# A decoder layer on one core: the first transfers in another order and on two queues, and the orders of all engines anew

## The chip, the cores and the metric

One core of a Trainium2 chip runs the whole program. The metric is the device time in microseconds (us). TensorE is called PE, VectorE DVE, ScalarE ACT, GpSimd POOL and SyncE SP, as in the profile.

## The reference

32 sequences of 128 tokens with 512 channels pass through one decoder layer in float32:

```python
x = x + _L0_attn_ref(_layernorm(x), ...)          # linear attention with decay, 32 heads of 16
x = x + _L0_xattn_ref(_layernorm(x), ctx, ctx)    # cross attention, 32 query heads, 8 key/value heads
x = x + _L0_ffn_ref(_layernorm(x), ...)           # feed-forward part with block-quantised operands
```

The attention part forms xx = (previous token - token), mixes it with a weight per channel into four inputs (`mix_r`, `mix_k`, `mix_v`, `mix_g`), projects each with a 512x512 weight, multiplies the scores of a head with powers of its decay, normalises the result per head, multiplies it with a gate silu(g) and projects it with Wo. The feed-forward part goes 512 to 2048 to 512 through a tanh-gelu. Its activations and both weights are quantised in blocks of 32 values with a shared exponent.

## The kernel before

One sequence is one tile of 128 tokens. All engines run at once, each through its own straight list of steps, and wait for each other with semaphores (`e.wait_ge`). The lists are written out by hand for sequences 0 to about 10 and for the last five. In between stands `for n in range(11, 27)` on every engine, so 16 turns of a loop in which one turn works on several sequences at different depths (the loading for n, the attention of n-1 and n-2, cross attention of n-3 and n-4, feed-forward of n-5 and n-6). The order of a list is the schedule: an engine stands still at a step whose wait isn't met, even when a later one could run.

Steps that matter here:
- `load_x`, `load_turned`: a sequence into `xin`, and the same transposed into `xt`.
- `stats_q(n)`, `norm_mv("q", n)` (DVE, L1623 to L1634), `rstd_log`, `rstd_exp` (ACT, L2655 to L2669): the first norm's two numbers per token, `norm_q`.
- `norms_out(n)` (L224) writes `norm_q` to a small tensor in DRAM, `row_norm`. `norms_to_all(n)` (L230) reads it back, as one row spread over all 128 partitions, into `norms`. Both are asked for by SP.
- `normalise_q(n)` (POOL, L3386, L3388) applies `norms` to `xt` and gives `xT`. `differences(n)` (DVE, L1655) gives `xx`, `mixed(n, name)` the four mixes (POOL: r and g, DVE: k and v).
- `project(name, n, ...)` (PE, L626), `project_v` (L616), `scores_r` (L645), `values_r` (L659, L664), `head_variance` (L672), `project_out` (L678): attention. `scores_max`, `scores_x`, `values_x` (L695, L710, L716): cross attention. `up` and `down` (L737, L746): feed-forward.
- The weights W1 and W2 come in 16 pieces of 128x1024 float32. Piece n is loaded (`load_w12`, into one of two stages; from n = 2 on it waits until piece n-2 is quantised), measured (`w12_scale`, DVE, L1841 and small ones), scaled (`w12_scaled`, POOL, L3437), quantised (`w12_quantise`, DVE, L1849, L1853) and turned by a transposing DMA (`w12_turned`, SP, L289).
- `distances`, `decays`, `bonuses`, `bonus_added` (L1860, L2796, L3446, L1866) build the table `wm` of powers that `decayed` (DVE, L1687) multiplies the scores with. `centre_values` (PE) and `centred` (ACT, L2800) fold a centring into Wv.
- ACT loads a table set when it changes between exp/log and gelu/tanh (ACT_TABLE_LOAD).

Of the kernel before, what the change touches and what calls it, by code (L numbers as in the profile page):

```python
# [11 lines left out]
ALU = mybir.AluOpType  # L12
ACT = mybir.ActivationFunctionType
AX_X = mybir.AxisListType.X

P = 128
# [39 lines left out]
def build(nc, x, x_turned, ctx_in, weights, w12, columns, rows, heads, b1, masks_in, out):  # L56
    with ExitStack() as ctx:
# [135 lines left out]

        @block.sync
        def _(e):
            def load(name, dst, src):
                e.dma_start(dst, src).then_inc(sem(f"sp_{name}"), 16)
# [19 lines left out]

            def norms_out(n):  # L220
                e.wait_ge(sem("act_rs_q"), 3 * n + 3)
                if n:
                    e.wait_ge(sem("sp_norms"), 16 * n)
                e.dma_start(row_norm[:, :], norm_q[:, :]).then_inc(sem("sp_row_norm"), 16)  # L224

            def norms_to_all(n):
                e.wait_ge(sem("sp_row_norm"), 16 * (n + 1))
                if n:
                    e.wait_ge(sem("pool_xT"), 2 * n)
                e.dma_start(norms[:, :, :].rearrange("p t k -> p (t k)"),  # L230
                            row_norm.rearrange("t k -> (t k)").unsqueeze(0).to_broadcast([P, 2 * T])).then_inc(sem("sp_norms"), 16)
# [77 lines left out]
            load_x(0)  # L309
            load("masks", masks[:, :], masks_in)  # L310
# [3 lines left out]
            load("Wo", wt["Wo"][:, :, :], weights["Wo"])  # L314
            load_w12(1)
            load("Wv", wv_rows, weights["Wv"])
            load_x(1)
            load("Wr", wt["Wr"][:, :, :], weights["Wr"])
            load("Wk", wt["Wk"][:, :, :], weights["Wk"])
            load("b1", b1row[:, :], b1)  # L320
            for k in ROWS:
                load("rows", row[k][:, :], rows[k])
            load("Wg", wt["Wg"][:, :, :], weights["Wg"])
            load_w12(2)
            w12_turned(0)
            load_w12(3)
            norms_out(0)
            load_turned(0)
            norms_to_all(0)
            w12_turned(1)  # L330
            w12_turned(2)
            load_w12(4)
            norms_out(1)
            load_w12(5)
            next_x(2)
            load_turned(1)
            norms_to_all(1)
            w12_turned(3)
            load_turned(2)
            load_w12(6)  # L340
            earlier_values(0)
            w12_turned(4)
            load_w12(7)
            w12_turned(5)
            load_w12(8)
            w12_turned(6)
            norms_out(2)
            norms_to_all(2)
            load_w12(9)
            earlier_values(1)  # L350
            load_ctx(0)
            w12_turned(7)
            load_ctx(1)
            next_x(3)
            queries_spread(0)
            load_w12(10)
            norms_out(3)
            load_turned(3)
            load_w12(11)
            w12_turned(8)  # L360
            w12_turned(9)
            maxima_to_rows(0)
            load_w12(12)
            load_w12(13)
            norms_to_all(3)
            w12_turned(10)
            earlier_values(2)
            load_ctx(2)
            w12_turned(11)
            even_sums(0)  # L370
            next_x(4)
            odd_outputs(0)
            load_w12(14)
            w12_turned(13)
            w12_turned(12)
            queries_spread(1)
            load_turned(4)
            load_w12(15)
            maxima_to_rows(1)
            w12_turned(15)  # L380
            w12_turned(14)
            norms_out(4)
            even_sums(1)
            norms_to_all(4)
            earlier_values(3)
            hidden_turned(0)
            odd_outputs(1)
# [4 lines left out]
            hidden_turned(1)  # L392
            load_turned(5)
            gelu_turned(0, 0)
            even_sums(2)
            norms_out(5)
            earlier_values(4)
            norms_to_all(5)
            gelu_turned(0, 1)
            next_x(6)  # L400
            odd_outputs(2)
            load_ctx(4)
            store(0)
            queries_spread(3)
            maxima_to_rows(3)
            gelu_turned(1, 0)
            load_turned(6)
            hidden_turned(2)
            norms_out(6)
            even_sums(3)  # L410
            earlier_values(5)
            norms_to_all(6)
            gelu_turned(1, 1)
            odd_outputs(3)
            next_x(7)
            load_ctx(5)
            queries_spread(4)
            store(1)
            maxima_to_rows(4)
            load_turned(7)  # L420
            norms_out(7)
            even_sums(4)
            hidden_turned(3)
            earlier_values(6)
            norms_to_all(7)
            gelu_turned(2, 0)
            gelu_turned(2, 1)
            next_x(8)
            odd_outputs(4)
            load_ctx(6)  # L430
            queries_spread(5)
            store(2)
            load_turned(8)
            maxima_to_rows(5)
            norms_out(8)
# [3 lines left out]
            earlier_values(7)  # L439
            norms_to_all(8)  # L440
            next_x(9)
            gelu_turned(3, 1)
            odd_outputs(5)
# [5 lines left out]
            norms_out(9)  # L449
            hidden_turned(5)  # L450
            even_sums(6)
            gelu_turned(4, 0)
            earlier_values(8)
            norms_to_all(9)
            next_x(10)
# [141 lines left out]
        def _(e):  # L597
# [22 lines left out]
            def project(name, n, bank, mixed_by):  # L620
                e.wait_ge(sem(f"{mixed_by}_mix{name}"), n + 1)
                if n == 0:
                    e.wait_ge(sem(f"sp_W{name}"), 16)
# [3103 lines left out]
```

## Time and profile before

| | us |
|---|---|
| median of 3 runs (lowest, highest) | 1369.63 (1363.61, 1373.9) |
| the profiled execution's own time | 1370.11 |
| its span, first to last instruction | 1368.3 |
| PE busy | 1236.5 |
| DVE busy | 1165.0 |
| ACT busy | 782.4 |
| POOL busy | 706.9 |

The span is what the rows below are read in. 1.8 us of the execution's time lie around it. An engine's busy time is the sum of its instructions without its waits; times in the rows count from the span's start.

### The profile page before, as it was taken

To read this page: it belongs to the slowest core of one execution; us is meant where nothing else is said; L and a number is where in the kernel's file an instruction comes from. 1 tells how busy PE (TensorE), PEld (TensorE's weight loads), DVE (VectorE), ACT (ScalarE), POOL (GpSimd) and SP (SyncE) were. 2 spreads that over 40 slices of the span, in tenths; PEclk is the share of its full clock that TensorE was granted. 3 is DMA by queue.
4 is the path that set the end of the run, shared out by engine and by line. 5 is a ranking of instruction groups with operands and counts; after the bars stand their busy time and mean duration, and the time that the engine had idled before them with its cause. 6 is when DMAs were issued, how large, how long until landed. Compare 5 with 4: busy or idle time off the path is not lost.

```text
span 1368.3 us, 37527 instructions
## 1 busy us (share of the span) xinstructions
PE 1236.5 (90%) x14729; PEld 778.9 (57%) x14760; DVE 1165.0 (85%) x1960; ACT 782.4 (57%) x1515; POOL 706.9 (52%) x764
## 2 busy tenths in 40 slices
PE   2477789999999999999999999999999999999844
PEld 2465555566666665666666666666666666556411
DVE  5788888988888888888888888888898998888875
ACT  2133465766756666666666666666666655556641
POOL 4775555445555555555554555555555554544322
PEclk9697999999999999999999999999999999999976
DMA  9565333322233333333222323333322222342212
GB/s 312 110 119 115 101 65 81 81 51 67 74 67 81 78 81 81 82 80 63 62 73 70 72 76 78 81 82 81 81 67 70 64 58 69 62 85 41 68 32 50
DMA packets 151166, 109.89 MB, mean 80 GB/s; under 512 B 113744, under 2 KB 119888, under 8 KB 150224
## 3 DMA queue, kind: packets, MB, share of 16 engines
q1 hardware_dynamic: 150992, 107.50, 33.0%
q8 instruction: 118, 1.93, 0.7%
q14 instruction: 56, 0.46, 0.2%
HBM read 49.75 MB, written 8.42 MB: 43 GB/s over the span
## 4 chain that ended last, share of the span: by engine, by line
PE 68%; DVE 12%; DMA 9%; issue 6%; POOL 3%; ACT 2%; SPq 1%; POOLq 0%; DVEq 0%; ACTq 0%
PE bank_b L626 14%; PE bank_a L626 7%; PE bank_y L678 7%; PE bank_a L616 7%; PE bank_y L746 5%; PE rt L710 4%; PE rt L645 4%; PE bank_o L716 4%; PE rt L695 4%; PE bank_b L737 3%; PE bank_a L737 3%; PE bank_o L672 2%; DMA gmem<-gmem 2%; DMA gmem<-w 2%; PE bank_y L664 2%
## 5 line engine op out<-in xcount | busy, mean ns | idle before, releaser
L3427 POOL TENSOR_TENSOR gmem<-gmem,unit_g 128x1024 bf16<-128x1024 bf16 x64 | 124.5, 1945 | 139.0 <-DVE unit_g L1769 139.0
L626 PE MATMUL bank_a<-mix_r,w_Wr 128*128 128x128 f32 x1024 | 128.6, 286 | 29.7 <-POOL mix_r L3376 29.7
L1716 DVE TENSOR_REDUCE negm<-rt 128x16 f32<-128x2048 f32 x64 | 145.1, 2268 | 9.8 <-PE rt L695 9.3
L3418 POOL TENSOR_TENSOR gt<-gt,yT 128x512 f32<-128x512 f32 x32 | 41.8, 1306 | 198.0 <-ACT yT L2737 198.0
L626 PEld LDWEIGHTS bank_a<-mix_r,w_Wr 128*128 128x128 f32 x1024 | 122.9, 200 | 33.5 <-POOL mix_r L3376 28.5
L746 PE MATMUL bank_y<-w2q,gmem 128*128 128x512 bf16 x481 | 118.0, 389 | 23.9 <-DMA gmem<-gmem 21.7
L2759 ACT ACTIVATE pT<-rt 128x2048 f32<-128x2048 f32 x64 | 120.1, 1877 | 28.1 <-PE rt L710 25.0
L626 PE MATMUL bank_b<-mix_g,w_Wg 128*128 128x128 f32 x1024 | 127.2, 284 | 7.1 <-DVE z_bf L1802 7.1
L626 PEld LDWEIGHTS bank_b<-mix_g,w_Wg 128*128 128x128 f32 x1024 | 121.5, 198 | 11.2 <-DVE z_bf L1802 8.0
L1687 DVE TENSOR_TENSOR att<-rt,wm 128x1536 f32<-128x1536 f32 x64 | 112.2, 1753 | 9.0 <-PE rt L645 8.9
L626 PE MATMUL bank_b<-mix_k,w_Wk 128*128 128x128 f32 x1024 | 119.8, 275 | 0.0
L626 PEld LDWEIGHTS bank_b<-mix_k,w_Wk 128*128 128x128 f32 x1024 | 118.5, 193 | 1.8 <-issue 1.8
L678 PE MATMUL bank_y<-w_Wo,yT 128*128 128x512 f32 x256 | 115.7, 594 | 0.7 <-DVE yT L1703 0.7
L616 PE MATMUL bank_a<-w_Wv,mix_v 128*128 128x512 f32 x256 | 115.4, 593 | 0.6 <-DVE mix_v L1662 0.6
L3386 POOL TENSOR_TENSOR xT<-xt,norms 128x512 f32<-128x512 f32 x32 | 41.4, 1294 | 114.4 <-DMA norms<-row_norm 114.4
L746 PEld LDWEIGHTS bank_y<-w2q,gmem 128*128 128x128 bf16 x512 | 49.7, 99 | 82.2 <-issue 24.9
L695 PE MATMUL rt<-context,qdense 32*64 32x256 f32 x2048 | 74.3, 399 | 13.9 <-DVE negm L1716 11.2
L645 PEld LDWEIGHTS rt<-rz,kT 32*64 32x64 f32 x3072 | 63.1, 131 | 36.2 <-issue 25.6
L616 PEld LDWEIGHTS bank_a<-w_Wv,mix_v 128*128 128x128 f32 x256 | 48.3, 190 | 61.6 <-issue 61.5
L1821 DVE SCALAR_TENSOR_TENSOR gmem<-gmem,pow_g 128x1024 bf16<-128x1024 f16 x64 | 81.9, 1281 | 1.0
L710 PE MATMUL rt<-qx,context 32*64 32x512 f32 x1024 | 74.0, 635 | 7.6 <-ACT pT L2759 2.8
L1757 DVE TENSOR_REDUCE amax_g<-gmem 128x32 f32<-128x1024 bf16 x64 | 77.5, 1211 | 2.5 <-ACT gmem L2791 2.5
(209 smaller groups left out, 2759.8 us busy)
## 6 DMA issues: line engine op xcount, KB each, us to landing
qx<-qdense SPq DMA_DIRECT2D x64, 224.0 KB, 3.7
context<-ctx SPq DMA_DIRECT2D x32, 384.0 KB, 3.5
xin<-x SPq DMA_DIRECT2D x32, 256.0 KB, 3.0
gmem<-w SPq DMA_DIRECT2D x16, 512.0 KB, 5.3
xt<-x_turned SPq DMA_DIRECT2D x32, 256.0 KB, 3.1
out<-x SPq DMA_DIRECT2D x32, 256.0 KB, 2.1
norms<-row_norm SPq DMA_DIRECT2D x32, 128.0 KB, 3.3
vp<-vz SPq DMA_DIRECT2D x32, 128.0 KB, 2.4
```

The source lines that it names most:

```text
L616: done = e.matmul(bank_a[:, :], mix["v"][:, c, :], wt["Wv"][:, c, :], start=(c == 0), stop=(c == KT - 1))
L626: done = e.matmul(bank[:, m * T:(m + 1) * T], wt[f"W{name}"][:, c, m * P:(m + 1) * P], mix[name][:, c, :], start=(c == 0), stop=(c == KT - 1))
L645: done = e.matmul(rtb(g)[HALF * side:HALF * side + HALF, at:at + (q1 - q0) * HALF], kT[rows32, m, HALF * keys:HALF * keys + HALF], rz[rows ...
L678: done = e.matmul(bank_y[:, :], yT[:, c, :], wt["Wo"][:, c, :], start=(c == 0), stop=(c == KT - 1))
L695: done = e.matmul(rtb(g)[half, jj * 2 * T:(jj + 1) * 2 * T], qdense[rows32, 2 * i + jj, half], kd[n % 2][rows32, :, :], start=True, stop=True)
L710: done = e.matmul(rtb(g)[half, :], kx[n % 2][rows32, i, half], qx[rows32, i, :, :], start=True, stop=True)
L737: done = e.matmul(bank[:, :], hqT[:, c, :], w1q[:, 4 * j:4 * j + 4, c, :], start=(c == 0), stop=(c == KT - 1))
L746: done = e.matmul(bank_y[:, :], gqT[:, t, :], w2q[:, t, :], start=(t == 0), stop=(t == FT - 1))
L1687: e.tensor_tensor(att[:, :, :, :, :].rearrange("p g m k t -> p g (m k t)"), rt[:, :].rearrange("p (g n) -> p g n", g=4)[:, :, 0:6 * HALF], ...
L1716: e.tensor_reduce(negm[:, 0:H].rearrange("p (g a j) -> p g j a", g=4, a=2)[:, :, 2 * i:2 * i + 2, :], rt[:, :].rearrange("p (g j a s) -> p ...
L2759: e.activation(pT[:, :, :].rearrange("p g n -> p (g n)"), rt[:, :], ACT.Exp, scale=float(D) ** -0.5).then_inc(sem(f"act_ex{i}"), 1)
L3427: e.tensor_tensor(blocks(half), blocks(half), per_block(unit[f"g{i}"], 32), ALU.mult).then_inc(sem(f"pool_gsc{i}"), 1)
```

## The change

`norms_out` and `norms_to_all` are moved out of SP's block and take the engine as an argument. For sequence 0 ACT asks for both, for all others still SP. Seven loads at the start (masks, columns, heads and weights) keep SP; `b1`, the four rows and `Wo` are asked for by ACT, later. `project_out(0)` gets a wait for `Wo`. DVE's opening steps become functions so that the first sequence's statistics can stand ahead of them. All the rest is a new order of the same steps on all engines, in front of the loop, in it and behind it.

```diff
+        def norms_out(e, n): ...        (was in SP's block; semaphores "norms", "row_norm")
+        def norms_to_all(e, n): ...
 SP, from the start
             load_x(0)
+            load_turned(0)
             masks, columns, heads, load_w12(0)
-            load("Wo", ...)
             load_w12(1)
             load("Wv", ...)
-            load_x(1)
             load("Wr", ...)
+            load_x(1)
             load("Wk", ...)
-            load("b1", ...); 4 x load("rows", ...)
             load("Wg", ...)
-            load_w12(2)
             w12_turned(0)
+            load_w12(2)
             load_w12(3)
-            norms_out(0); load_turned(0); norms_to_all(0)
             w12_turned(1)
...
 SP, loop
-                norms_out(n - 1)
                 hidden_turned(n - 5)
                 even_sums(n - 4)
+                norms_out(e, n - 1)
                 gelu_turned(n - 6, 0)
-                earlier_values(n - 2)
-                norms_to_all(n - 1)
+                norms_to_all(e, n - 1)
                 next_x(n)
+                earlier_values(n - 2)
                 gelu_turned(n - 6, 1)
 SP, sequence 31
+            norms_out(e, 31)
             hidden_turned(27)
             gelu_turned(26, 0)
-            norms_out(31)
+            earlier_values(30)
             even_sums(28)
-            load_turned(31); earlier_values(30); load_ctx(29)
-            norms_to_all(31)
+            norms_to_all(e, 31)
 PE, project_out
+                if n == 0:
+                    e.wait_ge(sem("load_Wo"), 16)
 PE, loop
                 turn_out(n - 4)
-                scores_max(n - 3, 0)
                 values_r(n - 2, 0)
+                scores_max(n - 3, 0)
 DVE, from the start (new order)
+            stats_q(0)
+            norm_mv("q", 0)
+            halved_columns(); rates_bounded()
+            distances(1); w12_scale(0); w12_scale(1); w12_quantise(0)
+            distances(0); w12_quantise(1); bonus_added(0)
+            w12_scale(2); w12_scale(3); w12_quantise(2)
+            stats_q(1); norm_mv("q", 1)
+            differences(0)
+            w12_quantise(3); mixed(0, "k"); w12_scale(4)
...
 DVE, loop
                 gelu_pow2(n - 5, 0)
+                stats_q(n)
                 up_out(n - 5, 3, bank_b)
-                stats_q(n)
...
                 hidden_round
+                gelu_quantised(n - 5, 0)
                 hidden_quantised
-                gelu_quantised(n - 6, 0)
-                gelu_max; scaled_y; spread_v; gated_y
+                spread_v; scaled_y; gelu_max; gated_y
 ACT, from the start (new order)
+            rstd_log("q", 0); rstd_exp("q", 0)
+            norms_out(e, 0)
+            rates()
+            norms_to_all(e, 0)
             decays(0); decays(1); centred()
+            later_loads()               # b1, 4 rows, Wo
 ACT, loop
                 queries_x(n - 3)
-                rstd_log("q", n)
-                gate_in(n - 2)
                 e.preload_act_table_set(TABLE_GELU)
                 gelu(n - 5, 3)
                 gate_tanh(n - 2)
+                e.preload_act_table_set(TABLE_EXP)
+                rstd_log("q", n)
+                gate_in(n - 2)
+                e.preload_act_table_set(TABLE_GELU)
                 gelu(n - 5, 2)
...
-                receptance(n - 1)       (now behind squares(n - 2))
 POOL, from the start
             bonuses(0)
+            normalise_q(0)
             w12_scaled(0); w12_scaled(1); bonuses(1); w12_scaled(2); w12_scaled(3)
-            normalise_q(0)
-            mixed(0, "r"); with_bias(0); w12_scaled(4); mixed(0, "g")
+            mixed(0, "g"); mixed(0, "r"); w12_scaled(4); normalise_q(1)
 SP, end
             gelu_turned(30, 1)
-            store(30)
             gelu_turned(31, 0); gelu_turned(31, 1)
+            store(30)
```

POOL's loop is unchanged. The other lists behind the loop are re-ordered in the same manner, by a step or two each.

## Rows read from the trace of the kernel before

**Rows 1.** The page's first part: busy time, share of the span, instructions.
```profile
PE 1236.5 (90%) x14729; PEld 778.9 (57%) x14760; DVE 1165.0 (85%) x1960; ACT 782.4 (57%) x1515; POOL 706.9 (52%) x764
```

**Rows 2.** Windows by stage: window, length, then busy us of each engine, clock, DMA.
```profile
0.00:50.90 50.90, 7.39 (x40) 7.23 (x40) 32.37 (x45) 8.44 (x12) 24.59 (x24) 0.77 0.90 252
50.90:205.00 154.10, 124.52 (x1547) 89.52 (x1551) 126.36 (x192) 62.72 (x137) 96.14 (x95) 0.89 0.48 99
...
411.00:1026.00 615.00, 613.33 (x7493) 387.02 (x7509) 543.17 (x952) 392.46 (x764) 331.34 (x377) 1.00 0.31 76
1026.00:1231.00 205.00, 195.12 (x2336) 124.67 (x2347) 181.75 (x292) 122.62 (x242) 107.29 (x118) 0.98 0.29 68
1231.00:1368.30 137.30, 94.87 (x922) 45.26 (x910) 99.61 (x172) 62.90 (x105) 41.49 (x33) 0.83 0.22 48
```

**Rows 3.** Timeline of the first 51 us: start, duration, instruction, idle before it.
```profile
4.71 0.17 DVE L1870 TENSOR_SCALAR half_bg<-all_columns 128x4 f32<-128x4 f32 x1 [4.71 <-DMA all_columns<-columns]
...
20.16 0.33 SPq L204 DMA_DIRECT2D gmem<-w  x1
...
32.50 1.22 DVE L1841 TENSOR_REDUCE amax_w<-gmem 128x32 f32<-128x1024 f32 x1 [8.84 <-DMA gmem<-w]
...
34.15 0.69 DVE L1623 BATCH_NORM_STATS2 stats_q<-xin 128x6 f32<-128x512 f32 x1
...
36.03 0.33 SPq L224 DMA_DIRECT2D row_norm<-norm_q  x1
...
43.62 1.28 POOL L3386 TENSOR_TENSOR xT<-xt,norms 128x512 f32<-128x512 f32 x1 [4.75 <-DMA norms<-row_norm]
...
50.92 5.75 PE L626 MATMUL bank_a<-mix_r,w_Wr 128*128 128x128 f32 x32 [28.35 <-POOL mix_r L3376]
```

**Rows 4.** DMA of the first 60 us: issues, KB each, median us to landing.
```profile
w_Wg<-Wg SPq DMA_DIRECT2D x1, 1024.0 KB, 21.5
```

**Rows 5.** The instructions that touch `row_norm`, whole span: landing of both legs.
```profile
DMA to landing us min/median/max: 3.0/3.3/5.4
```

**Rows 6.** Timeline of POOL's and DVE's work on weights at the start.
```profile
14.98 3.34 POOL L3437 TENSOR_TENSOR gmem<-gmem,unit_w 128x1024 f32<-128x1024 f32 x1 [0.43 <-DVE unit_w L1769]
...
99.77 1.22 DVE L1853 SCALAR_TENSOR_TENSOR hz<-gmem,pow_w 128x1024 bf16<-128x1024 f32 x1
```

**Rows 7.** DVE's waits from 50 to 210 us: total, times, longest.
```profile
DVE amax_w L1841 <- DMA gmem<-w: 6.8, 4, 3.5
...
DVE hz L1853 <- DMA w2q<-hz: 3.0, 1, 3.0
```

**Rows 8.** One turn of the loop, timeline: SP's first gelu transpose, ACT's table load, first project.
```profile
672.04 1.24 SPq L302 DMA_TRANSPOSE gmem<-gmem  x1
...
690.91 1.28 ACT L3085 ACT_TABLE_LOAD   x1
...
704.14 1.23 SPq L296 DMA_TRANSPOSE hqT<-hz  x1
...
708.99 1.04 PE L737 MATMUL bank_b<-w1q,hqT 128*128 128x512 bf16 x4
```

**Rows 9.** DMA from 420 to 1030 us: the transposes of h, median us to landing.
```profile
hqT<-hz SPq DMA_TRANSPOSE x16, 2.5
```

**Rows 10.** SP's first gelu transpose of later turns (one of two per turn).
```profile
1047.07 1.24 SPq L302 DMA_TRANSPOSE gmem<-gmem  x1
...
1207.20 1.23 SPq L302 DMA_TRANSPOSE gmem<-gmem  x1
1208.53 0.55 SPq L224 DMA_DIRECT2D row_norm<-norm_q  x1
...
1213.39 0.38 SPq L230 DMA_DIRECT2D norms<-row_norm  x1
...
1249.40 1.31 SPq L302 DMA_TRANSPOSE gmem<-gmem  x1
```

**Rows 11.** PE's waits from 1030 to 1230 us.
```profile
PE bank_b L626 <- DVE z_bf L1802: 5.8, 4, 2.6
```

More of the change, by code:

```diff
@@ L192, in build, with norms_out, norms_to_all @@
         block = ctx.enter_context(nc.Block())
+        def norms_out(e, n):
+            e.wait_ge(sem("act_rs_q"), 3 * n + 3)
+            if n:
+                e.wait_ge(sem("norms"), 16 * n)
+            e.dma_start(row_norm[:, :], norm_q[:, :]).then_inc(sem("row_norm"), 16)
+        def norms_to_all(e, n):
+            e.wait_ge(sem("row_norm"), 16 * (n + 1))
+            if n:
+                e.wait_ge(sem("pool_xT"), 2 * n)
+            e.dma_start(norms[:, :, :].rearrange("p t k -> p (t k)"),
+                        row_norm.rearrange("t k -> (t k)").unsqueeze(0).to_broadcast([P, 2 * T])).then_inc(sem("norms"), 16)
         @block.sync
@@ L338, in _ @@
-            w12_turned(3)
-            load_turned(2)
[L340 to L345, printed above, removed]
-            w12_turned(6)
[L347 to L351, printed above, removed]
+            norms_to_all(e, 1)
+            load_w12(6)
+            w12_turned(4)
+            earlier_values(0)
+            w12_turned(5)
@@ L359, in _ @@
-            load_w12(11)
-            w12_turned(8)
+            load_w12(12)
+            maxima_to_rows(0)
+            w12_turned(10)
             w12_turned(9)
-            maxima_to_rows(0)
-            load_w12(12)
             load_w12(13)
[L365 to L368, printed above, removed]
+            norms_out(e, 3)
+            norms_to_all(e, 3)
             w12_turned(11)
             even_sums(0)
+            load_turned(3)
@@ L522, in _ @@
             gelu_turned(24, 0)
-            norms_out(29)
-            norms_to_all(29)
-            earlier_values(28)
+            norms_out(e, 29)
+            norms_to_all(e, 29)
             gelu_turned(24, 1)
@@ L792, in _ @@
             scores_r(1, 1)
-            e.wait_ge(sem("dve_Ra1"), 2)
-            scores_x(0, 0)
+            e.wait_ge(sem("dve_x1"), 1)
+            values_r(1, 0)
+            e.wait_ge(sem("act_rT"), 3)
+            project_v(2)
             values_r(1, 1)
@@ L1990, in _ @@
             mixed(4, "k")
+            maxima(2, 0)
+            stats_q(5)
+            up_out(0, 2, bank_a)
             stats_f(1)
-            norm_mv("f", 1)
-            maxima(2, 0)
-            up_out(0, 2, bank_a)
-            stats_q(5)
             norm_mv("q", 5)
@@ L2885, in _ @@
             gate_in(3)
+            values_copied(3)
+            gelu(0, 3)
             gate_tanh(3)
[L2887 to L2893 removed]
             gelu(0, 2)
@@ L2896, in _ @@
             rstd_log("q", 5)
-            squares(3)
+            rstd_log("f", 1)
+            rstd_exp("q", 5)
+            maxima_turned(2)
+            rstd_exp("f", 1)
+            normalise_f(1)
             rstd_log("g", 1)
             rstd_exp("g", 1)
+            squares(3)
+            receptance(4)
+            head_log(3)
+            head_rstd(3)
             weights_x(2, 0)
-            rstd_exp("q", 5)
-            head_log(3)
-            receptance(4)
-            head_rstd(3)
+            keys_r(4)
+            out_even(2)
             weights_x(2, 1)
-            out_even(2)
-            keys_r(4)
             e.preload_act_table_set(TABLE_GELU)
@@ L3156, in _ @@
             maxima_turned(25)
+            normalise_f(24)
             rstd_exp("q", 28)
-            normalise_f(24)
-            receptance(27)
             rstd_log("g", 24)
@@ L3219, in _ @@
             rstd_exp("f", 26)
+            normalise_f(26)
             maxima_turned(27)
-            normalise_f(26)
-            receptance(29)
             rstd_exp("q", 30)
```

1087 lines of the change are left out of this document (540 added, 547 removed).

## The prediction

> **What bounds the kernel now.** I read the busy times first. PE is at 90% of the span and DVE at 85% [rows 1], so neither a share of time nor a busy engine says where the rest lies. Windows by stage do [rows 2]. From 411 to 1026 us PE is busy 613.3 of 615.0 us at a full clock: there PE is the bound, and no order makes it shorter, since the same matmuls are left. PE stands idle 43.5 us before its first projection at 50.9 us (50.9 - 7.4), 29.6 us from there to 205, 9.9 us from 1026 to 1231 and 42.4 us after that, which is 125.4 of the 131.8 us in which it is idle at all. The change can only win there. The timeline of the first 51 us [rows 3] says what the beginning waits for: DVE's fourth list entry measures piece 2 of W1, whose load was asked for at 20.16 us behind some 9 MB of other loads and was there at 32.50. The first norm's statistics stand behind it, at 34.15, although its sequence was asked for first of all. Then come 0.29 + 0.20 + 0.29 us on ACT, the two DMA legs through DRAM from 36.03 to 43.62, and 7.3 us of POOL and DVE up to PE's start at 50.92.
>
> **The change, part by part.** All sums are made against the profiled execution, 1370.1 us, which is 0.5 us over the median shown.
>
> *First norm.* Its statistics now stand first on DVE. The columns, asked for third, were there at 4.71 us [rows 3], so the sequence is there by then and `norm_q` about 1.7 us later, at 6.4. Two legs follow. In the rows one leg takes 3.0 to 5.4 us, median 3.3 [rows 5]; the trip before took 7.6 us from 36.03 to 43.62 [rows 3]. Now they run beside the first loads, at 0.90 DMA share over this stage [rows 2]. Wg, last in SP's list of loads, took 21.5 us to land [rows 4], which is a leg's upper bound should it have to queue like that; I take 10 us for both, nearer to 7.6, since they go on a queue that holds nothing else. `norms` would be there at 16.4, against 43.62.
>
> This case shows no queue of ACT's beside a full one of SP's. The Trainium skill (DMA: Bandwidth & Descriptors, Queues, rings and completion order) says that each DMA engine takes turns between the queues at packet granularity, which would make the trip short; the same section says that the write that signals completion lands only after every earlier write of that DMA engine, across its queues, which speaks against the change. By the first rule alone the trip would be nearer to 7.6 us. By the second it would lengthen, and that is the second rival below.
>
> *What is late next.* Little of these 27 us arrives at PE, since `differences(0)` still stands on DVE behind the measuring of pieces 2 and 3. Piece 2's load waits until piece 0 is quantised, which waits for POOL's scaling of it, which now stands behind `normalise_q(0)`. Step by step: `norms` 16.4; `xT` 1.3 + 1.4 us, 19.1; scaling 1.9 to 3.3 us [rows 6], 21.7; quantising 2.0, 23.7; the load asked for behind one transpose issue at 25.0 and landed after 5, at 30.0 (12.3 before, when the queue was full [rows 3]; the queue now holds some 3 MB less, as b1, the rows and Wo are asked for after `centred`, about 31). Pieces 2 and 3 measured, piece 2 scaled and quantised, statistics of sequence 1: 7.6 us, 37.6. `differences(0)` 0.7; then POOL makes `mix_g` before `mix_r`, 2.85 us more than before, so 5.7 in all. PE's first projection: 44, against 50.92. That is **-7**. Bounds: 40 with a trip of 7.6 us and the short scaling; 52, a loss of 1, with 18 us for the trip. Table `wm` is finished later (ACT stands at `norms_to_all(0)` with `decays` and `centred` behind it), but it is first needed by `decayed(0, 0)`, which ran at 62.7 and will at 58; if `centred` came after 50 it would hold `project_v(0)`.
>
> *To 205 us.* At PE's start one bonus step (1.75 us) and about 1.2 us of measuring are still to do on DVE that were done before: **+3** at most. Against that, DVE waited 6.8 us for pieces of weights and 3.0 us for a transpose [rows 7], because a piece was measured too soon after the one that frees its stage. In the new list only piece 6 stands so. The others have 4 us or more of work between. Of these 9.8 us I take 6: **-6**. Between are the waits for PE's scores, which move with PE. Two marks: piece 8 was quantised from 98.9 and its last step began at 99.77 [rows 6]; following the list by hand I get 90 to 91. Bounds for both terms together: 0 (all is DVE's 126.4 of 154.1 us of work, and what it gained it loses again for other releasers) and -12.
>
> *The loop.* From 672.04 [rows 8] to 1047.07 [rows 10] ten turns take 375.0 us, 37.5 each. `stats_q` ahead of `up_out(., 3)` costs nothing, since `project("g")` came 1.2 us after it. `values_r` ahead of `scores_max` delays `maxima` by 1.1 us, covered by work of the same length. ACT gets one more pair of table loads, 2 x 1.28 us [rows 8], with room: it is busy 392.5 of 615 us [rows 2]. The pair puts `rstd_log("f")` about 1.2 us later and `normalise_f` 0.7 us, and `gelu_quantised` ahead of `hidden_quantised` 1.2 us, so that the transpose of h is asked for at 706.0 instead of 704.14. It takes 2.5 us [rows 9], which gives 708.5 against 708.99 when PE wants it [rows 8]. `receptance` behind `squares` ends just as `project_v` wants its bank. So all is just covered. I take 0.1 us a turn, **+2** over the 16 turns and the neighbours; bounds -1 and +10 (0.6 a turn, both covers missed).
>
> *Behind the loop.* From 1047.07 to 1249.40 five turns take 202.3 us, 14.8 more than five of the loop [rows 10]. PE's only wait of weight there is for DVE's `z_bf` [rows 11], which stood behind `differences`, which waited for the norms. For sequence 31 `norms_out` was asked for at 1208.53 behind a gelu transpose and `norms_to_all` at 1213.39 behind three more loads [rows 10]; now the first goes ahead and the loads away, about -3. For 30 nearly nothing changes, as `norms_to_all` now stands behind `load_ctx(28)`. **-3**; bounds +4 and -8. At the end DVE has `second_out(30)` and `residual(30)` behind the last gelu, 1.1 us off the final path: **-1**, bounds +2 and -4.
>
> Sum: -7 + 3 - 6 + 2 - 3 - 1 = -12; 1370.1 - 12 = 1358. About 1% (13.7 us) is what a measurement of this kernel can tell from no change, so this lies at the border.
>
> **Rivals.** (a) *All goes well*: the trip takes 7.6 us, PE starts at 40, the waits for weights go, and the turns behind the loop lose half as much: 1370 - 11 - 8 - 7 - 1 = 1343. For it speaks how much idle time lies in these stages [rows 2], against it that DVE is busy 82% there.
> (b) *The round trip is slow under load.* ACT's two small transfers wait on the same DMA engines as the loads: 18 us or more for both. POOL and ACT stand at it, piece 0 is scaled late, and PE starts at 51 or later. Only a few us of the later waits are left: 1370 + 1 - 3 + 2 - 4 = 1366. For it: the DMA share of 0.90, and 12.3 us for piece 2's load in that time [rows 3].
> (c) *The loop's cover is gone*, the one on the slower side. The transposed h comes after PE wants it, by the two table loads and the quantising put ahead. At 1.3 us a turn: 16 x 1.3 = 21, instead of 2: 1370 - 14 + 21 = 1377. It decides from 0.85 us a turn on, where it eats the other terms. For it: only 0.5 us of cover is left by my count. Against it: DVE has 71.8 us idle over 615 [rows 2], 4.4 a turn.
> (d) *The change doesn't do what it says*: the early norm is there, but the list puts the wait elsewhere. That is in the sum.
>
> **How the numbers follow.** Forecast 0.40, (a) 0.25, (b) 0.20, (c) 0.15. The forecast's own range is 1350 to 1366. The range from (a) to (c), opened for the bounds: 1338 to 1377. Below 1356.4 the kernel is faster by over 1%: all of (a), half of the forecast but for little of (b), 0.45. Over 1383.3 it is slower by over 1%: a third of (c), and what nobody's list counts, 0.10. The rest, 0.45, is within 1%.
>
> **What would show it.** `stats_q(0)` at about 4 us and `norms` landed at 14 to 19 us; PE's first projection (L626 before) near 44 us; DVE's wait for piece 2 still there but from about 27 to 30 us; PE's idle time before 205 us down from 73 to about 60; a turn of 37.5 to 37.6 us, without PE waits for `hqT`. The prediction is wrong if a turn takes over 38 us, if the first projection comes before 38 or after 50, or if PE's idle time moves from the beginning to the stage of 100 to 200 us, where DVE is the second bound.

## The result: slower by 2.5%, and the profile after

| | before | after |
|---|---|---|
| median of 4 runs (lowest, highest), us | 1370.91 (1363.61, 1373.9) | 1403.12 (1399.81, 1410.94) |
| ratio, with its 95% interval | | 1.0251 [1.0192, 1.031] |
| the profiled execution, us | 1370.11 | 1403.7 |
| its span, us | 1368.3 | 1401.9 |

The forecast was 1358 with a range of 1338 to 1377: the sign was wrong and the time lies 26 us outside the range. All medians and ratios here are of executions with a mean granted clock of 0.95 or more; one execution of the eighth kernel below, 1880.16 us at a clock of 0.627, is left out.

The windows by stage of the kernel after, with the same columns and bounds as in [rows 2] (the last one is longer by the loss):

```profile
0.00:50.90 50.90, 7.49 (x40) 7.32 (x40) 28.73 (x41) 8.21 (x12) 20.84 (x22) 0.76 0.77 239
50.90:205.00 154.10, 121.28 (x1504) 85.14 (x1505) 132.26 (x191) 58.09 (x129) 92.77 (x95) 0.90 0.47 104
...
411.00:1026.00 615.00, 591.45 (x7172) 368.45 (x7171) 527.86 (x917) 415.22 (x764) 325.16 (x361) 1.00 0.34 72
1026.00:1231.00 205.00, 194.09 (x2402) 122.25 (x2402) 178.38 (x295) 132.21 (x252) 108.97 (x122) 0.99 0.31 70
1231.00:1401.90 170.90, 129.91 (x1301) 66.06 (x1299) 135.42 (x225) 84.05 (x145) 60.80 (x52) 0.89 0.21 52
```

PE's idle time in the stretch from 411 to 1026 us went from 1.7 us to 23.6 us, at a full clock. PE was the bound there; now something else is. Windows are cut at fixed times, so I read where the time went from a mark that every sequence has, the issue of the transpose of h (`hqT<-hz`), counted from 0:

| stretch by that mark | before | after | |
|---|---|---|---|
| start to the fifth issue, us | 329.8 | 334.7 | +4.9 |
| fifth to 23rd (the loop and its neighbours, 18 turns) | 674.5 | 710.1 | +35.6 |
| 23rd to the end of the span | 363.9 | 357.0 | -6.9 |
| one turn, mean of 14 in the middle of these (8th to 22nd issue) | 37.54 | 39.02 | +1.48 |

So the loss is the loop, there is a small loss at the start, and the end gains. These stretches are of one profiled execution of each kernel. The chain of the kernel after, over one turn of the loop, in order of time (start, us, what):

```profile
693.87 0.61 ACT odense L2770
...
694.49 0.61 SPq L263
...
695.20 3.27 DMA row_norm<-norm_q
...
698.49 4.31 DMA norms<-row_norm
...
702.86 1.30 POOL xT L3403
...
704.24 1.30 POOL xT L3405
...
705.56 1.75 DVE xx L1651
...
707.34 1.14 DVE mix_k L1658 x4
...
708.79 0.11 DVE stats_q L1619
...
709.39 0.68 DVE z_bf L1798
...
710.12 3.84 PE bank_b L620 x32
...
731.26 1.04 PE bank_o L712 x8
...
732.33 0.61 ACT odense L2770
```

It closes on itself: a cycle over the turns. `values_x` (L712) gives ACT's `odense`. SP's `even_sums` (L263) waits for that, and `norms_out` now stands behind it. Two DMA legs, POOL's `xT`, DVE's `xx`, `mix_k`, `stats_q` and `z_bf` follow, then PE's `project("g")`, 22 us of PE, and `values_x` again: 732.33 - 693.87 = 38.46 us, longer than PE's own 37.5. The two legs hold 19.6% (10.9 and 8.7) of the chain from 411 to 1026 us; the chain of the kernel before is PE's matmuls there and neither leg is among its named lines. SP's timeline of that turn shows the order:

```profile
691.32 1.23 SPq L296 DMA_TRANSPOSE hqT<-hz  x1
694.49 0.61 SPq L263 DMA_DIRECT2D oden<-odense  x1
695.20 0.39 SPq L198 DMA_DIRECT2D row_norm<-norm_q  x1
695.69 1.36 SPq L302 DMA_TRANSPOSE gmem<-gmem  x1
698.49 0.33 SPq L204 DMA_DIRECT2D norms<-row_norm  x1
```

In the kernel before, `norms_out` of such a turn was issued at 698.17, ahead of the transpose of h at 704.14 [rows 8], so the first leg had 13 us until `norms_to_all` was issued at 711.41. But `norms_to_all` stood behind `even_sums` there too. The way round existed before, with one leg in it instead of two:

```profile
708.71 0.63 SPq L263 DMA_DIRECT2D oden<-odense  x1
...
711.41 0.55 SPq L230 DMA_DIRECT2D norms<-row_norm  x1
...
715.00 1.29 POOL L3386 TENSOR_TENSOR xT<-xt,norms 128x512 f32<-128x512 f32 x1 [3.40 <-DMA norms<-row_norm]
...
716.37 1.29 POOL L3388 TENSOR_TENSOR xT<-xT,norms 128x512 f32<-128x512 f32 x1
...
719.23 0.68 DVE L1655 TENSOR_TENSOR xx<-xT 128x512 f32<-128x512 f32 x1
...
721.40 0.68 DVE L1802 SCALAR_TENSOR_TENSOR z_bf<-bank_b,b1row 128x512 bf16<-128x512 f32 x1
...
723.27 3.84 PE L626 MATMUL bank_b<-mix_g,w_Wg 128*128 128x128 f32 x32
```

POOL waited for the norms in every turn, but PE didn't, as this way had slack in two places: `xx` ran 1.57 us after `xT` was there (717.66), and `project("g")` 1.19 us after `z_bf` (722.08). That is 2.76 us, not 13. The turn of the kernel after, from the two listings above, uses up more than that:

| part of the way round, us | before | after | |
|---|---|---|---|
| `even_sums` to `norms_to_all` issued | 2.70 | 4.00 | +1.30 |
| `norms_to_all` issued to POOL's `xT` | 3.59 | 4.37 | +0.78 |
| DVE's `xx` | 0.68 | 1.74 | +1.06 |
| `stats_q` ahead of `z_bf` | 0 | 0.60 | +0.60 |
| slack at `xx` and at `project("g")` | 2.76 | 0.09 | -2.67 |

The last column adds up to 1.07 us, and from `odense` to `odense` this turn took 38.46 us against 37.40 (708.08 to 745.48).

The timeline of the first 56 us, which answers to [rows 3]:

```profile
3.39 0.69 DVE L1619 BATCH_NORM_STATS2 stats_q<-xin 128x6 f32<-128x512 f32 x1 [3.39 <-DMA xin<-x]
...
5.35 0.35 ACTq L198 DMA_DIRECT2D row_norm<-norm_q  x1
...
14.40 0.33 ACTq L204 DMA_DIRECT2D norms<-row_norm  x1
...
22.11 1.27 POOL L3403 TENSOR_TENSOR xT<-xt,norms 128x512 f32<-128x512 f32 x1 [12.68 <-DMA norms<-row_norm]
...
26.64 2.38 DVE L1845 TENSOR_SCALAR gmem<-gmem 128x1024 f32<-128x1024 f32 x1 [11.90 <-POOL gmem L3454]
...
37.61 1.22 DVE L1837 TENSOR_REDUCE amax_w<-gmem 128x32 f32<-128x1024 f32 x1 [2.13 <-DMA gmem<-w]
...
47.54 0.68 DVE L1651 TENSOR_TENSOR xx<-xT 128x512 f32<-128x512 f32 x1
...
55.11 5.20 PE L620 MATMUL bank_a<-mix_r,w_Wr 128*128 128x128 f32 x23 [34.32 <-POOL mix_r L3393]
```

The statistics came early, but the two legs took 9.05 and 7.7 us. POOL stood 12.68 us at `xT` with piece 0's scaling behind it, and DVE stood 11.90 us for that scaling. `xx` ran at 47.54 although `xT` was there at 24.7, and PE's first projection came at 55.11, against 50.92 before.

### The profile page after: what moved, and what is told of

It reads as the page before. It is cut to its first block, busy times and chain, and to the rows that moved or that the text cites. A ratio compares the mean times of both kernels' runs of the same rounds, so it can differ in the third digit from the quotient of the medians.

```text
span 1401.9 us, 37590 instructions
## 1 busy us (share of the span) xinstructions
PE 1240.5 (88%) x14760; PEld 775.3 (55%) x14760; DVE 1175.5 (84%) x1960; ACT 822.5 (59%) x1547; POOL 712.3 (51%) x764
## 4 chain that ended last, share of the span: by engine, by line
PE 44%; DVE 19%; DMA 19%; issue 7%; POOL 7%; SPq 2%; ACT 1%; POOLq 0%; DVEq 0%; ACTq 0%
PE bank_b L620 12%; DMA norms<-row_norm 7%; PE bank_a L620 6%; DMA row_norm<-norm_q 6%; PE bank_a L610 6%; DVE xx L1651 3%; PE bank_y L674 3%; PE rt L639 2%; PE rt L691 2%; PE rt L706 2%; POOL xT L3405 2%; POOL xT L3403 2%; PE bank_o L712 2%; DVE mix_k L1658 2%; DMA gmem<-w 2%
## 5 line engine op out<-in xcount | busy, mean ns | idle before, releaser
L742 PE MATMUL bank_y<-w2q,gmem 128*128 128x512 bf16 x512 | 125.6, 391 | 24.0 <-DMA gmem<-gmem 23.8
L620 PE MATMUL bank_b<-mix_g,w_Wg 128*128 128x128 f32 x1024 | 124.3, 280 | 22.5 <-DVE z_bf L1798 22.5
L3435 POOL TENSOR_TENSOR gt<-gt,yT 128x512 f32<-128x512 f32 x32 | 52.1, 1629 | 169.6 <-ACT yT L2739 169.6
L620 PEld LDWEIGHTS bank_b<-mix_g,w_Wg 128*128 128x128 f32 x1024 | 118.4, 194 | 26.8 <-DVE z_bf L1798 24.8
L2793 ACT ACTIVATE gmem<-z_bf 128x512 bf16<-128x512 bf16 x64 | 40.3, 629 | 91.4 <-DVE z_bf L1798 67.9
L2713 ACT ACTIVATE gt<-bank_b,half_bg 128x128 f32<-128x128 f32 x128 | 36.5, 370 | 85.5 <-PE bank_b L620 85.5
L610 PEld LDWEIGHTS bank_a<-w_Wv,mix_v 128*128 128x128 f32 x256 | 47.7, 190 | 63.0 <-issue 47.4
L733 PE MATMUL bank_b<-w1q,hqT 128*128 128x512 bf16 x256 | 68.2, 390 | 14.4 <-DMA hqT<-hz 12.1
```

Source lines behind the costliest of these rows:

```text
L610: done = e.matmul(bank_a[:, :], mix["v"][:, c, :], wt["Wv"][:, c, :], start=(c == 0), stop=(c == KT - 1))
L620: done = e.matmul(bank[:, m * T:(m + 1) * T], wt[f"W{name}"][:, c, m * P:(m + 1) * P], mix[name][:, c, :], start=(c == 0), stop=(c == KT - 1))
L733: done = e.matmul(bank[:, :], hqT[:, c, :], w1q[:, 4 * j:4 * j + 4, c, :], start=(c == 0), stop=(c == KT - 1))
L742: done = e.matmul(bank_y[:, :], gqT[:, t, :], w2q[:, t, :], start=(t == 0), stop=(t == FT - 1))
```

## The experiments

Fifteen kernels ran. Ratios are to the kernel before on the same chip. "h4", "loop" and "end" are the three stretches of the table above, of one profiled execution each, which can lie several us off the median: that of kernel 13 is its fastest (1354.98 against 1361.83), that of kernel 9 is 5 us below its median and that of kernel 12 is 4 us above. Kernels 1 to 4 ran on one chip, 5 to 8 on a second, 9 to 12 on a third, 13 to 15 on a fourth.

**1. The loop's order on SP: undone alone, done alone, and its two companions.** The first kernel is the changed one with

```diff
 SP, loop
+                norms_out(e, n - 1)          (head of the turn)
                 ...
                 even_sums(n - 4)
-                norms_out(e, n - 1)
```

> The changed kernel with one line of SP's loop moved: norms_out(n-1) asked for at the head of the turn again, ahead of hidden_turned and even_sums. Theory A (the first norm's way through DRAM closes a cycle over the turns: odense of cross attention, SP's even_sums, norms_out, two legs, xT, xx, mix_k, z_bf, the projection g, and PE's work down to the next odense): the cycle is cut, a turn goes from 39.0 back to about 37.5 us and the time falls by 16 to 18 turns x 1.5 to 1.9, to 1370 to 1378. Theory B (ACT's two more table loads and the transposed h that comes late set the turn): no change, 1400 to 1406.

The second is the kernel before with the opposite edit, `norms_out(n - 1)` moved from the head of the turn to behind `even_sums(n - 4)`.

> The kernel before with the same one line moved the other way: in SP's loop norms_out(n-1) stands behind even_sums(n-4). All else as before. Theory A: the cycle is closed here too. It is shorter than in the changed kernel by DVE's stats_q (0.69 us), which stands behind z_bf here, and longer by earlier_values (0.54 us) ahead of norms_to_all: a turn of 38.0 to 38.6 us, 1379 to 1390 in all. Theory B: 1370, no change.

The third is the changed kernel without the added pair of table loads in ACT's loop (`rstd_log("q", n)` and `gate_in(n - 2)` ahead of `gelu(n - 5, 3)` again).

> The changed kernel with ACT's loop free of the extra pair of table loads (rstd_log q and gate_in ahead of the gelus again, as before). Theory A: the turn stays at 39.0 and the time within 4 us of 1403. Theory B: ACT and with it h come 1 to 1.3 us earlier, the turn falls to about 37.6 and the time to 1378 to 1385.

The fourth is the changed kernel with DVE's `stats_q(n)` behind `up_out(n - 5, 3, bank_b)`, which makes `z_bf`, as before.

> The changed kernel with DVE's stats_q(n) behind up_out(n-5, 3) again. Theory A: stats_q's 0.69 us leaves the cycle, 16 turns x 0.69 = 11 us, 1392. Theory B: no change, since z_bf of piece 3 is not what PE waits for, 1403 give or take 3.

| kernel | median us | ratio | h4 | loop | end | norms legs, median us |
|---|---|---|---|---|---|---|
| changed | 1403.12 | 1.0251 [1.0192, 1.031] | 334.7 | 710.1 | 357.0 | 3.9 |
| 1 changed, `norms_out` first | 1378.17 | 1.0081 [1.006, 1.0103] | 335.7 | 679.6 | 360.5 | 3.2 |
| 2 before, `norms_out` late | 1375.03 | 1.0061 [1.0042, 1.0079] | 326.9 | 685.7 | 363.4 | 3.6 |
| 3 changed, no table pair | 1389.02 | 1.0159 [1.0119, 1.0199] | 333.2 | 695.5 | 355.5 | 3.8 |
| 4 changed, `z_bf` first | 1384.38 | 1.0132 [1.0103, 1.0162] | 336.7 | 688.4 | 357.5 | 3.5 |

One line of SP's list, put back, leaves a loop stretch of 679.6 us, 30.5 less than in the changed kernel's profile, and the legs leave the chain of the loop. (Against the changed kernel as kernel 9 ran it below, with 693.8, it is 14.2 less.) The time, 1378.17, is the upper end of the expectation. The same line, moved alone in the kernel before, adds 11.2 us to that stretch and puts both legs into the chain (8.6% and 6.1% of it), but that is a third of the loss, and 1375.03 is below the 1379 us at which the expectation began. So the line is enough to use up the slack, and other parts of the change lengthen the way further. The fourth kernel shows one of them, as `stats_q` lies in the cycle ahead of `z_bf`: PE's waits for `z_bf` from 411 to 1026 us fall from 13.9 us to 0.9. Its time, 1384.38, is below both expectations (1392 and 1400 to 1406). The third contradicted the theory: it should have stayed within 4 us of 1403 and came out 14 us faster, though not as fast as theory B had it either. How far such times scatter for one and the same program shows in the next group, and by that the sizes in kernels 3 and 4 can't be told.

**2. Loop mended, the start, and the changed kernel again.** The fifth kernel joins edits 1, 3 and 4.

> The changed kernel with the three loop edits of the first round together: norms_out at the head of SP's turn, no extra pair of table loads on ACT, stats_q behind up_out. Theory A (cycle through the norms, closed by SP's order and lengthened by stats_q; the table pair costs a second, smaller cover): the turn is 37.5 us as before, 1403 less 28 to 36: 1367 to 1375. What is left to the kernel before is the start (5 us later) and the part behind the loop (7 us shorter). Rival: a further cause in the loop (DVE's order of spread_v, or values_r ahead of scores_max) keeps it at 1376 to 1380.

The sixth is the changed kernel with POOL's order at the start mended:

```diff
 POOL, from the start
             bonuses(0)
-            normalise_q(0)
             w12_scaled(0); w12_scaled(1)
+            normalise_q(0)
```

> The changed kernel with one POOL step moved at the start: normalise_q(0) behind w12_scaled(0) and w12_scaled(1). Theory S1 (the start is late because the weight pieces wait behind POOL's wait for the slow norms): piece 0 is quantised at about 18 instead of 29, piece 2 lands near 27, PE's first projection comes at 45 to 48 instead of 55.1, and the time falls by 5 to 9 us to 1394 to 1398. Rival S2 (the pieces wait for the DMA engines, not for POOL): the first projection stays at 54 or later, 1401 to 1405.

The seventh is the changed kernel with SP waiting for `norms` of sequence 0 before it asks for the first piece of W1, so that the trip runs beside almost no loads.

> The changed kernel with SP waiting for the norms of sequence 0 before it asks for any weight (w12 pieces, Wv, Wr, Wk, Wg). Theory Q1 (the two legs took 9.05 and 7.7 us because they share the DMA engines with 5 MB of loads): the legs take 3 to 4.5 us each, the norms land at about 12.5 instead of 22.1. Rival Q2 (ACT's queue, or the first use of it, is slow itself): 9 and 7.7 us stay. For the time: the weights come 9 us later, so the first projection comes at 46 to 52 and the time is 1394 to 1404.

The eighth is the kernel before with the early first norm alone, and used: the statistics first, both legs asked for by ACT, the turned sequence second on SP, `b1`, rows and `Wo` later, and `differences(0)` and the mixes ahead of pieces 2 and 3.

> The kernel before with the early first norm alone, and used: statistics of sequence 0 first on DVE, both legs on ACT's queue, xt loaded second, b1, the rows and Wo later; and, unlike in the changed kernel, differences(0) and the mixes of sequence 0 stand ahead of the measuring of pieces 2 and 3 on DVE, and normalise_q(0) behind the scaling of pieces 0 and 1 on POOL. Loop and tail are those of before. Theory S3 (the idle 8.8 us of DVE and 28 us of PE at the start can be used): first projection at 28 to 31 instead of 50.9, 8 to 12 us off: 1355 to 1360. Rival S4 (from 50 to 205 us DVE's work sets the pace and what is gained comes back): 1366 to 1370.

The ninth is the changed kernel without any edit, on the chip of the next group.

> The changed kernel once more, beside the next three. Theory D (the loop can run at two paces, and the changed kernel's start puts it into the slower one): again 1398 to 1410 with a turn of 39.0. Rival F (the two paces belong to the chip of the run and its DMA times, since the loops of this kernel and of e6 are the same): beside e6 on one chip it lies 8 to 12 us above it, which is what the start alone is worth, 1380 to 1384.

| kernel | median us | ratio | h4 | loop | end |
|---|---|---|---|---|---|
| 5 loop mended | 1375.96 | 1.0083 [1.0053, 1.0113] | 331.8 | 682.9 | 359.0 |
| 6 POOL scales first | 1372.24 | 1.0052 [1.0033, 1.0071] | 322.7 | 691.0 | 356.9 |
| 7 loads behind norms | 1376.2 | 1.0093 [1.007, 1.0116] | 324.6 | 692.2 | 356.8 |
| 8 before, norm early and used | 1363.93 | 0.9994 [0.9979, 1.0009] | 329.0 | 674.1 | 359.1 |
| 9 changed again | 1391.97 | 1.0195 [1.0146, 1.0243] | 334.6 | 693.8 | 356.7 |

The ninth matters for all the others. The same program took 693.8 us in the loop stretch in its profile, against 710.1 on the first occasion. The kernel before moved by 5 us only, 1370.91 to 1365.97. Between 400 and 1040 us the time from `even_sums` to the issue of `norms_to_all`, which holds the first leg, was 3.68 us in the median against 3.99, and the time from there to POOL's `xT`, the second leg, 4.30 against 4.55. That is 0.56 us of the 0.72 by which the mean turn was shorter (38.30 against 39.02): a cycle with two DMA legs in it takes on the legs' duration. Kernels 6 and 12 are one program too, 1372.24 and 1381.26, where the kernel before took 1364.70 and 1365.97. The 14 us of the third kernel are therefore not shown to be a price of the table pair: its loop stretch of 695.5 is near the ninth's 693.8, with the pair. Kernels 3, 4, 6 and 7 still have both legs behind `even_sums`, so their loop stretches carry this scatter; kernels 1 and 5 don't have that in the loop.

The expectations that counted from 1403 missed, in good part for this reason. Kernels 6 and 7 were expected at 1394 to 1398 and 1394 to 1404 and came about 20 us lower, and the ninth lies between the 1398 to 1410 of theory D and the 1380 to 1384 of rival F. Kernel 5 came just above its 1367 to 1375.

At the start, the sixth kernel's trip took as long (5.59 to 22.82 us) but nothing of the weights stood behind it: its first projection came at 44.64 us, 10.5 us earlier, and its h4 12 us earlier. That is also 7.1 us ahead of the kernel before (322.7 against 329.8): with that one step of POOL moved, the change's new start gains. The seventh shows what made the trip long. Its timeline:

```profile
5.39 0.35 ACTq L198 DMA_DIRECT2D row_norm<-norm_q  x1
8.31 0.33 ACTq L204 DMA_DIRECT2D norms<-row_norm  x1
...
12.38 1.28 POOL L3404 TENSOR_TENSOR xT<-xt,norms 128x512 f32<-128x512 f32 x1 [2.84 <-DMA norms<-row_norm]
```

Without the megabytes beside them the same legs on the same queue take 2.9 and 4.1 us, 7.0 in all instead of 16.8. A queue of its own didn't keep the trip short while the loads ran.

The eighth answers what the change's first idea is worth. Its first projection came at 33.07 us, 17.9 us before that of the kernel before. Its first transpose of h was issued at 179.1 us, against 179.5, and its time is that of the kernel before, where 1355 to 1360 had been expected. PE's earlier start only meets later waits. DVE, which has the weight pieces to quantise in that time, is busy 140.50 of the 172 us from 33 to 205; that it sets the pace there fits this, but no run takes it apart. The early norm alone gains nothing here.

**3. Both mends together.** The tenth kernel joins edits 6, 1 and 4; the eleventh adds that SP asks for Wv only when `norms` of sequence 0 has landed; the twelfth is the sixth again, on the same chip as the ninth.

> The changed kernel with three steps moved: normalise_q(0) behind the scaling of pieces 0 and 1 (POOL, start), norms_out at the head of SP's turn, stats_q behind up_out on DVE. If the two causes add up (12 us of start, cycle in the loop), it takes 322.7 us to the fifth transpose of h, 675 to 680 for the 18 turns and 357 after that: 1356 to 1361, 0.2 to 0.6% below the kernel before. Rival: PE is the bound of the loop whatever the start, and the start's gain is lost to waits later, 1364 or more.

> As e10, and SP asks for Wv, Wr, Wk and Wg only when the norms of sequence 0 are there (pieces 0 and 1 still ahead of them). The legs take 3 to 5 us each with 1.3 MB of loads on the way, the norms land at about 13 to 16. Theory S3 (the start gains by early norms): a further 1 to 3 us, 1354 to 1359. Rival S4 (weights are what the start waits for): 0 to 3 us worse than e10.

> The kernel of e6 (one POOL step moved at the start) once more, so that it and the changed kernel stand side by side. Theory D: 1368 to 1373 again, 30 us below the changed kernel on the same chip, of which the start explains 12. Rival F: 8 to 12 us below it.

| kernel | median us | ratio | h4 | loop | end |
|---|---|---|---|---|---|
| 9 changed again, same chip | 1391.97 | 1.0195 [1.0146, 1.0243] | 334.6 | 693.8 | 356.7 |
| 10 POOL, SP and DVE mended | 1368.66 | 1.0008 [0.9982, 1.0034] | 324.5 | 684.7 | 359.6 |
| 11 the same, Wv waits | 1372.61 | 1.0053 [1.0019, 1.0087] | 328.4 | 683.1 | 358.1 |
| 12 POOL alone, again | 1381.26 | 1.0104 [1.0054, 1.0155] | 322.1 | 700.2 | 361.2 |

On one chip, mending POOL's start alone is worth 10.7 us (12 against 9) and SP's and DVE's loop another 12.6 (10 against 12). The tenth was expected at 1356 to 1361 and missed that; it is 1364 or more, as its rival said. In the eleventh the first leg took 5.2 us instead of 9.0 (issued at 5.46 and 10.66), but the weights came later: its first projection came at 48.13 us, against 44.33 in the tenth, and instead of gaining 1 to 3 us it stands 4 us above it, with intervals that overlap. A shorter trip bought with later loads gains nothing here. But the tenth's loop stretch was still 10 us above that of the kernel before, with a turn of 37.57 in the middle. Its two slowest turns were at the front, 41.7 and 42.7 us between the fifth, sixth and seventh issue, where the kernel before took 36.6 and 38.4. The chain in them goes through the same legs:

```profile
329.86 3.55 DMA row_norm<-norm_q
...
333.43 4.22 DMA norms<-row_norm
```

The hand-written turns 7 to 9 and 26 to 28 hold the same move, and I had mended the loop alone.

**4. The order of `norms_out` everywhere.** The thirteenth kernel is the tenth with `norms_out` ahead in the turns for 7, 8, 9, 26, 27 and 28 too. The fourteenth is the changed kernel with that alone, on SP, in the loop and the six turns. The fifteenth is the thirteenth without the pair of table loads.

> As e10, and norms_out ahead of hidden_turned and even_sums in six turns written out by hand too (sequences 7, 8, 9, 26, 27, 28). Theory A2 (the 10 us that e10 still loses between the fifth and the 23rd transpose of h, 684.7 against 674.5, are the same cycle in the turns before the loop): that stretch falls to 675 to 678 us and the time to 1358 to 1362, under the kernel before. Rival G (these turns lose through the filling of the pipe or DVE's order): it stays at 683 or more and the time at 1366 to 1370.

> The changed kernel with SP's norms_out alone moved ahead, in the loop and in the same six turns. All else as changed, with the slow start. Theory A2: the loop stretch takes 675 to 679 us instead of 710.1 and 693.8, the start stays 5 us late: 1370 to 1374. Rival: the ACT table pair and stats_q cost their own time, 1376 or more.

> As e13 without ACT's extra pair of table loads in the loop. Theory A2: the pair only mattered while the cycle was closed; here within 2 us of e13. Rival B2: it has a price of its own of 0.2 us a turn or more, 3 us or more below e13.

| kernel | median us | ratio | h4 | loop | end |
|---|---|---|---|---|---|
| 13 all mended | 1361.83 | 0.9971 [0.9956, 0.9986] | 321.6 | 678.5 | 353.1 |
| 14 SP's `norms_out` alone | 1370.28 | 1.0029 [1.0012, 1.0047] | 333.8 | 676.6 | 358.1 |
| 15 the 13th, no table pair | 1360.11 | 0.9964 [0.9949, 0.9978] | 325.2 | 677.8 | 354.5 |

Seven lines of one list, each moved by one to three places, bring the changed kernel from 1.0195 to 1.0251 (two occasions) down to 1.0029, at a time within the expectation, and the loop stretch to 676.6 us, 2.1 above the kernel before. The thirteenth and fifteenth came within the expected times too. Three views of the middle of the run. The instructions that touch `row_norm` in the fourteenth kernel, from 420 to 1000 us:

```profile
DMA to landing us min/median/max: 3.0/3.3/4.4
```

Its `xx` in the same stretch, from the list of groups (busy us, mean ns of one, idle before):

```profile
L1651 DVE TENSOR_TENSOR xx<-xT 128x512 f32<-128x512 f32 x16 | 10.9, 681 | 0.0
```

The window of the thirteenth kernel, with the columns of [rows 2]:

```profile
411.00:1026.00 615.00, 610.45 (x7530) 388.27 (x7545) 527.08 (x948) 431.31 (x798) 339.08 (x381) 1.00 0.31 75
```

PE is busy 610.45 of 615 us again. With POOL's start and DVE's `stats_q` mended as well, the kernel beats the one before by 0.3%, and without the table pair by 0.4%; both intervals lie below 1, and the difference of these two, 1.7 us, isn't told apart from nothing.

## Why the prediction was wrong, point by point

*The loop* (+2, bounds -1 to +10; measured +35.6). This is the step that failed. It costed `stats_q`, `values_r`, ACT's table pair, `gelu_quantised` and `receptance`, and it left out the one line of the diff that moves `norms_out(n - 1)` on SP from the head of the turn to behind `even_sums(n - 4)`. I asked what each move delays by its own duration, and a DMA issue of 0.4 us has none to speak of. What I should have asked is what the issue now waits for: `even_sums` waits for ACT's `odense`, so for PE's cross attention of this turn, and `norms_out` waits with it. Undoing it in the loop and in the six turns beside it (kernel 14) leaves 2.1 of the 35.6 us; against the changed kernel as kernel 9 ran it, 17.2 of 19.3 us are given back. The kernel before did show where to look: POOL waited there for `norms` in every turn (47.7 us in 15 waits from 420 to 1000 us), behind the same `even_sums`, and from there to PE the way had 2.76 us of slack in the turn shown above. The first leg's 13 us were the only large slack on it, and the moved line gave them up. The landings in [rows 5] are those of the second leg alone; the first has none on record in the kernel before.

What I named as the cover that might go, the transposed h, was no part of it. Rival (c) had the right side and nearly the right size a turn (1.3 us; measured 1.48), but by a mechanism that the runs don't bear out: in the window of 420 to 1000 us PE waited for `hqT` for 3.3 us in two waits, and without the table pair the kernel isn't measurably faster (15 against 13).

```profile
PE bank_b L620 <- DVE z_bf L1798: 12.7, 13, 1.4
...
PE bank_y L742 <- DMA gmem<-gmem: 4.0, 6, 1.5
...
PE bank_b L733 <- DMA hqT<-hz: 3.3, 2, 1.9
```

These rows are PE's waits of the kernel after. The first, 13 times, is the cycle's door to PE. `stats_q` ahead of `up_out(., 3)` "costs nothing, since `project("g")` came 1.2 us after it" was right for the move alone (kernel 14 has it, with a median turn of 37.4 us) and wrong in this list: that slack existed only while the norms came early, and the late norms used it up.

*The first norm's trip* (10 us, bounds 7.6 to 18; measured 16.8). The mechanism was named as rival (b) with "18 us or more" and the price within its bounds. I took the value near 7.6 because the queue holds nothing else; the seventh kernel shows that the queue isn't what counts. By the Trainium skill (DMA: Bandwidth & Descriptors, Queues, rings and completion order) the engines take turns between queues at packet granularity, which by itself doesn't foretell 9.05 us for 1 KB; its other rule, that completion waits for every earlier write of the DMA engine, fits, but no run here tells that from plain queueing behind the loads.

*PE's first projection* (-7, at 44; measured +4.2, at 55.11). The chain that I wrote down, POOL's scaling behind `normalise_q(0)`, then piece 2's load behind that, is the one that the timeline shows, later by more at each step: `norms` 5.7 us (22.1 for 16.4), quantising 6.6 (30.3 for 23.7), piece 2 7.6 (37.6 for 30.0), `xx` 9.9 (48.2 for 38.3, piece 3 having landed only at 41.4), the projection 11.1. So half of the miss is the trip, and half the small delays behind it, which I had all taken at their shortest. The bound of 52 for a trip of 18 us was too low for that reason.

*To 205 us* (+3 - 6). DVE's wait for pieces of weights fell from 6.8 [rows 7] to 4.0 us, and the first transpose of h came 3.9 us later than before where the first projection came 4.2 later. So the two terms together are about 0, their upper bound. The eighth kernel shows that an earlier start of PE needn't arrive at the end of this stretch, so these terms don't add up as I added them; that DVE sets the pace there is argued, not shown. The sixth kernel's 12 us fit that: what it gives back is DVE's 11.90 us of standing still. With that the start gains 7.1 us over the kernel before, where -7 + 3 - 6 = -10 had been forecast.

*Behind the loop and at the end* (-3 - 1; measured -6.9). The side was right. From the 29th issue of the transpose of h to the 32nd it took 90.2 us against 93.2, from there to the end 27.7 against 29.5, and the six turns before these took 2.1 us less in sum. What I gave as the reason isn't shown: PE's wait for `z_bf` went from 5.8 us [rows 11] to 4.8 us (from 1030 to 1260 us) only. No experiment took this part apart.

*The sum.* +4.9 + 35.6 - 6.9 = 33.6, the difference of the spans. (The two 1% marks in the chances, 1356.4 and 1383.3, start from two values, 1370.1 and 1369.63; nothing hangs on that.) The marks that I set for being wrong were the right ones, a turn over 38 us and a first projection after 50, and both came.

## What to carry to other kernels

When an in-order list is re-ordered, ask of every moved issue not what it costs but what the steps now ahead of it wait for, and then follow its result round to see whether it comes back to the same place one turn later. If such a cycle closes, add it up, find the slack along it, and compare it with the bound engine's turn. A wait on an engine that isn't the bound, like POOL's for the norms, tells that the way is in use, and the slack lies behind it. Here the moved leg and what came with it added 3.74 us to a way that had 2.76 us of slack in the turn shown, and made the time depend on the occasion. Here too, a queue of its own didn't make a small transfer quick beside megabytes of loads (16.8 us against 7.0 for both legs): put nothing that others need behind such a landing.

## What the runs showed of the hardware

A DVE subtraction of 128x512 float32 took 0.68 us alone and 1.74 us when a POOL operation ran beside it. The timeline of the kernel after:

```profile
705.49 1.27 POOL L3424 TENSOR_TENSOR xin<-xin,r_bo 128x512 f32<-128x512 f32 x1
705.56 1.74 DVE L1651 TENSOR_TENSOR xx<-xT 128x512 f32<-128x512 f32 x1 [0.46 <-POOL xT L3405]
```

In the kernel before and in the fourteenth the norms come earlier, POOL is through with `xT` and with the operation behind it before DVE gets to `xx`, and all 16 take 0.68 us. The late norms so added a further 1.06 us to the cycle. The subtraction ends at 707.30, 0.54 us after POOL's operation at 706.76, so it did nearly nothing before that. The Trainium skill (SBUF — State Buffer, SBUF: two separate sides) says the same: a DVE operation with two SBUF inputs and a GpSimd operation that reads SBUF need one shared pair of ports, which the first of them holds for the whole instruction. These rows agree, and I hadn't counted it.

The second leg, `norms<-row_norm`, took 4.5 us in the median in the changed loop, and 3.1 to 3.2 in the kernel before and in kernels 1 and 14, with `norms_out` ahead. A gelu transpose is issued just ahead of it in all of them, so that alone doesn't explain it; what does stays open. For one and the same program the first leg took 3.3 us in the median in the first profile and 2.9 in kernel 9's; what sets that stays open too.
